# Attention's value product: key tile 0 in two blocks of 256 queries, a wait for masks at each block, query projection one unit sooner

## The reference, cut to what matters

```python
q = (x @ Wq + bq).reshape(Bb, Ss, H, HD)
k = (x @ Wk + bk).reshape(Bb, Ss, H, HD)
v = (x @ Wv + bv).reshape(Bb, Ss, H, HD)
scores = jnp.einsum('bthd,bshd->bhts', q, k) / jnp.sqrt(jnp.asarray(HD, x.dtype))
scores = scores + alibi[None]
scores = jnp.where(causal[None, None], -jnp.inf, scores)
attn = jax.nn.softmax(scores, axis=-1)
out = jnp.einsum('bhts,bshd->bthd', attn, v).reshape(Bb, Ss, Dd)
return out @ Wo + bo
```

## Time and profile before

| what | value |
|---|---|
| median of 3 runs | 937.36 us (935.0, 937.36, 949.56) |
| the profiled execution's own time | 934.77 us |
| its span, first to last instruction | 933.1 us |
| PE busy | 828.5 us (89%), 6498 matmuls |
| DVE busy | 752.8 us (81%) |
| ACT busy | 640.4 us (69%) |
| POOL busy | 537.4 us (58%) |
| mean granted TensorE clock | 0.951 |

### The profile page before, as it was taken

The page is one execution under the profiler, slowest core; times in us unless marked ns, Lnnn a source line. Parts: engine busy times, 40 slices in busy tenths (PEclk is TensorE's granted clock), DMA queues, the critical chain, the costliest instruction groups (busy, mean ns, idle before and its releaser), DMA issues. The chain is left out here.

```text
span 933.1 us, 23978 instructions
## 1 busy us (share of the span) xinstructions
PE 828.5 (89%) x6498; PEld 383.2 (41%) x6498; DVE 752.8 (81%) x2534; ACT 640.4 (69%) x1538; POOL 537.4 (58%) x838
## 2 busy tenths in 40 slices
PE   4999999359899999999999999999999977999997
PEld 3444444124334444444434444444444334444443
DVE  3899988348788888988988988888899416999996
ACT  3776666211687778778778778777877844766775
POOL 3677777431654654655565565475453323778787
PEclk9999999655899999999999999999999997999999
DMA  6500000042221322232232232132221001000101
GB/s 165 106 0 0 0 0 0 34 153 87 99 94 65 124 104 69 104 108 80 85 122 82 70 134 91 62 121 103 73 101 36 2 3 22 28 30 26 30 26 43
DMA packets 57044, 62.50 MB, mean 67 GB/s; under 512 B 6752, under 2 KB 50656, under 8 KB 56864
## 3 DMA queue, kind: packets, MB, share of 16 engines
q1 hardware_dynamic: 56992, 61.86, 20.5%
HBM read 32.23 MB, written 29.36 MB: 66 GB/s over the span
## 5 line engine op out<-in xcount | busy, mean ns | idle before, releaser
L1094 DVE TENSOR_REDUCE att_neg_max<-att_max 128x1 bf16<-128x512 f32 (+3 forms) x704 | 414.5, 638 | 61.8 <-PE att_max L888 59.5
L987 ACT ACTIVATE att_probs<-att_exp 128x512 f32<-128x512 f32 x640 | 357.6, 596 | 102.4 <-PE att_exp L907 98.5
L1059 POOL TENSOR_SCALAR_AFFINE_SELECT att_probs<-att_probs 128x512 f32<-128x512 f32 x256 | 159.0, 634 | 240.9 <-ACT att_probs L987 240.8
L907 PE MATMUL att_exp<-att_q_st,att_k_st 53*128 53x512 bf16 (+3 forms) x1024 | 223.0, 302 | 0.6 <-ACT att_probs L987 0.6
L885 PE MATMUL att_max<-att_k_st,att_q_st 51*128 51x384 bf16 (+2 forms) x768 | 191.2, 285 | 19.4 <-DVE att_neg_max L1094 11.4
L923 PE MATMUL att_pv<-att_probs,att_v 128*32 128x512 f32 (+3 forms) x2048 | 191.8, 448 | 2.7 <-POOL att_probs L1059 2.4
L360 ACT ACTIVATE moe_scaled<-moe_hi,moe_gates 128x128 f32<-128x128 f32 x512 | 145.7, 371 | 61.4 <-PE moe_hi L306 61.0
L520 DVE SCALAR_TENSOR_TENSOR x<-moe_lo,moe_gates,x 128x128 f32 (+1 forms) x512 | 160.7, 339 | 20.3 <-PE moe_lo L300 19.2
L888 PE MATMUL att_max<-att_k_st,att_q_st 64*128 64x128 bf16 x1024 | 176.0, 224 | 0.0
L885 PEld LDWEIGHTS att_max<-att_k_st,att_q_st 51*128 51x128 bf16 x768 | 71.1, 95 | 216.4 <-DVE att_neg_max L1094 159.1
L300 PE MATMUL moe_lo<-moe_we,moe_hT 128*128 128x512 f32 x256 | 136.0, 613 | 0.0
(11 more groups left out here) (81 smaller groups left out, 872.1 us busy)
## 6 DMA issues: line engine op xcount, KB each, us to landing
qk_parts<-att_parts SPq DMA_DIRECT2D x32, 384.0 KB, 2.7
att_q_st<-qk_parts SPq DMA_DIRECT2D x64, 192.0 KB
att_k_st<-qk_parts SPq DMA_DIRECT2D x64, 192.0 KB
qk_parts<-att_parts SPq DMA_DIRECT2D x32, 256.0 KB, 2.1
x<-in_L_attn_x SPq DMA_DIRECT2D x16, 256.0 KB, 2.9
qk_parts<-att_parts SPq DMA_DIRECT2D x32, 128.0 KB, 1.7
out<-x SPq DMA_DIRECT2D x16, 256.0 KB, 2.3
moe_we<-in_L_ffn_We SPq DMA_DIRECT2D x2, 512.0 KB, 4.9
```

What stands on the lines that cost most here:

```text
L907: mm = nc.tensor.matmul(exp_ps[m % RING][:, c:c + S - j * P], k_st[par][low:low + FINE_ROW, r, j * P:(j + 1) * P], q_st[par][low:low + FIN ...
L987: nc.scalar.activation(probs[g % 2][:, n, :], exp_ps[m % RING][:], ACT.Exp).then_inc(exp_done, 1)
L1059: nc.gpsimd.affine_select(out=view, in_=view, compare_op=ALU.is_ge, fill=0.0, base=0, pattern=[[0, 4], [1, P]], channel_multiplier=-1).the ...
L1094: nc.vector.tensor_reduce(neg_max[par][:, g // 2, 1 - g % 2, heads[0]:heads[0] + len(heads), i], max_ps[m % RING][:, 0:len(heads) * width] ...
```

## The change

The block of key tile 0 (512 queries) becomes two blocks of 256: queries 0 to 255 behind unit 2 and 256 to 511 behind unit 3. The first block of each key tile waits for `masked` up to the number in `MASKED_FOR`: 1 for key tile 0, 3 for tile 1, 4 for tile 2, 3 for tile 3; the second block of key tile 0 has no wait. Only the very first matmuls (key tile 0, queries from 0, first head of a pair) have the start flag. `project_q` goes from unit 2 to unit 1 of group 0. Nothing else changes.

```diff
 SIDE_WORK = [
-    {2: "project_q", 4: "shift_hi", 8: "project_k"},
+    {1: "project_q", 4: "shift_hi", 8: "project_k"},
...
-PV_AFTER = {3: 0, 5: 1, 7: 2, 9: 3}
+
+PV_AFTER = {2: (0, 0, 2), 3: (0, 2, 4), 5: (1, 1, 4), 7: (2, 2, 4), 9: (3, 3, 4)}
+MASKED_FOR = [1, 3, 4, 3]
...
-                            on_pv(b, par, g - 1, PV_AFTER[n])
+                            on_pv(b, par, g - 1, *PV_AFTER[n])
                         if g == 0 and there(b - 1):
-                            on_pv(b - 1, 1 - par, GROUPS - 1, PV_AFTER[n])
+                            on_pv(b - 1, 1 - par, GROUPS - 1, *PV_AFTER[n])
...
-            def weigh_values(b, par, g, j):
+            def weigh_values(b, par, g, j, q0, q1):
 
                 half_at, ab = divmod(g, 2)
-                if j == 0:
-                    pe.wait_ge(masked, b * NK + (g + 1) * MASK_UNITS)
+                if q0 == j:
+                    pe.wait_ge(masked, b * NK + g * MASK_UNITS + MASKED_FOR[j])
+                if j == 0 and q0 == 0:
                     if ab == 0 and (g > 0 or after(b, 0)):
                         pe.wait_ge(pv_read, b * HALVES + half_at)
                     if g == 0:
                         pe.wait_ge(side_read, use(b - 1, "project_v"))
                 for hh in range(4):
                     n, c = next((n, c) for n in range(EXP_UNITS) for h, jj, c in exp_unit(n) if (h, jj) == (hh, j))
-                    mm = nc.tensor.matmul(pv_ps[VW * hh:VW * (hh + 1), j * P:S], v[par][:, j, 4 * half_at + hh, ab, :],
-                                          probs[g % 2][:, n, c:c + S - j * P], start=(ab == 0 and j == 0),
-                                          stop=(ab == 1 and j == T - 1))
+                    mm = nc.tensor.matmul(pv_ps[VW * hh:VW * (hh + 1), q0 * P:q1 * P], v[par][:, j, 4 * half_at + hh, ab, :],
+                                          probs[g % 2][:, n, c + (q0 - j) * P:c + (q1 - j) * P],
+                                          start=(ab == 0 and j == 0 and q0 == 0), stop=(ab == 1 and j == T - 1))
                 if j == T - 1:
                     mm.then_inc(pv_out, 1)
...
-            def copy_values(b, par, g, j):
+            def copy_values(b, par, g, j, q0, q1):
```

## The result

The changed kernel takes 950.0 us (median of 4 runs, 948.87 to 950.83), the kernel before on the same chip 936.18 (4 runs). The ratio is 1.0179, 95% interval 1.0151 to 1.0207: slower by about 16.7 us, where I had forecast 8.7. The ratio leaves out one execution of the kernel before (949.56) that ran in the chip's slower state; the median of all four has it in. The profiled execution took 950.72 us with a span of 949.0, against 934.77 and 933.1.

A forecast was written before the change was run, and what follows sets the result against it. The prediction took PE to set the pace in groups 0, 1 and 3 and DVE in group 2. Its terms, 9.9 - 0.9 + 0.7 - 1.0 = +8.7 us on 934.8, gave 943.5 us, range 932 to 951.

The forecast's parts named there:

- split, walks 0 to 14: Key tile 0's two half blocks on PE: 0.66 us a walk in groups 0, 1 and 3, 9.9 us over 15 walks.
- masks in group 1: Unit 3 to its block in group 1: 0.09 us of mask waiting goes in about 10 walks, -0.9 us.
- more waits: Own waits for key tiles 1, 2 and 3 on PE's queue: taken as 0, with 0.09 kept for the range.
- `project_q`: Query projection behind unit 1 instead of 2 in group 0: same matmul between the same neighbours, cost 0.
- last walk and end: Last walk pays +0.66 us in three groups; at the end key tile 0 moves into the mask wait, -1.0 us.
- +0.22 us a group on PE: Units 2 and 3 with key tile 0's block go from 1.54 to 1.76 us; group 2's stall absorbs it.
- The waits show (slower): Three more waits a group on PE's queue cost 0.09 us each, 17.3 us over 192, giving 964; chance 0.07.
- no stall worth a row: Groups 1 and 3: PE's blocks follow each other without notable stall, so PE sets the pace from unit 2 on.
- Rows 1: The page's strip over attention, slices 10 to 32: read as PE at 9 in every slice, clock granted in full.
- Every group pays: Group 2 pays too, so all 64 groups cost 0.22 us: +12.2, 947 us; chance 0.12.
- nearly free: The half blocks' fixed part overlaps its neighbours, so only the gains stay: 933 us; chance 0.09.
- evening out: Parting projection and long block in group 0 ends DVE's 0.95 us of waits a walk: 929 us; chance 0.12.

The follow-up runs named there:

- slots 0 and 40: Changed kernel with PE's loop loaded so its first instruction is number 0 or 40 of a block of 256 instructions: 932.18 us and 931.98 us.
- `project_q` alone: Kernel before with only the query projection moved from behind unit 2 to behind unit 1: 933.78 us, ratio 0.9999.
- slot 236: Kernel before, only PE's loop loaded to start at instruction 236 of a block of 256: 943.13 us, ratio 1.0132.
- finer waits alone: Kernel before with each key tile waiting for its own masks; key tile 0 one block behind unit 3, query projection at unit 2: 927.05 us, ratio 0.9915.
- the kernel before with its loop written out: Kernel before with PE's loop over walks written out, so no jump back, and nothing else: 929.65 us, ratio 0.9964.
- slot 64: Changed kernel, only PE's loop loaded to start at instruction 64 of a block of 256: 939.68 us, ratio 1.0086.
- the split with one wait: Changed kernel without separate mask waits: key tile 0's first block waits behind unit 2 for all four masks: 964.43 us, ratio 1.0334.
- the run with the loop written out: Changed kernel with PE's loop over walks written out, other engines still in loops: 931.69 us, ratio 0.9979.

## Why the prediction was wrong

The time of 950.0 lies within the range, near its end, but for another reason than any case in it, so that it lies there is luck. The forecast and what the traces show, in us (walks are counted by the sequence whose values they weigh; all terms but the code's compare the kernel before with the change at slots 0 and 40):

| term | forecast | measured |
|---|---|---|
| split, walks 0 to 14 (measured: 1 to 14) | +9.9 | +4.7 |
| masks in group 1 | -0.9 | 0 |
| masks at the start (walk 0) | none | -3.7 |
| more waits | 0 | 0 |
| `project_q` (the walk ahead of walk 0 alone) | 0 | +0.2 |
| last walk and end | -0.3 | -0.9 |
| **code fetched at the jump back** | **none** | **+18.2** |
| sum in attention | +8.7 | +18.5 |

From the first max unit to the last value product attention takes 582.3 us instead of 563.8. Between the two profiled executions it also began 2.4 us sooner (195.6 instead of 198.0); the run of the change at slot 0 begins at 198.1 and that of `project_q` alone at 195.8, so that is no part of the change. 18.5 - 2.4 gives the 16 us between them.

**The step that failed** is the price of the split, "+0.22 us a group on PE", and with it the whole sum, which has no term for added instructions but the time that they run. "More waits ... only its handling on PE's queue counts" has the same gap, though its 16 instructions alone did no harm (927.05 us). 128 of the 144 added to the loop's body are the split's. What the runs showed in its place is 18.2 us at four jumps back, which go away (932.18) when the same body is loaded at another place. The order that I had read showed the growth (the query projection stood at 879 and now at 893, although it comes a unit sooner; the last products at 1755 and now at 1806). No rival held it. The rival "The waits show (slower)" had the right direction and the wrong mechanism: the leads before key tiles 1 to 3 did not grow (mostly 0.40, 0.32 to 0.37 and 0.21 us, before and after). The Trainium skill ("Runtime: NRT & Kernel Launch", section "Instruction fetch mechanics") says that PE's instruction memory holds 2048 instructions in blocks of 256, fetched ahead in sequence, and that a taken branch out of the current window of two pages costs a fetch. I had not weighed it. The runs agree with the eight blocks and with the block's size (258 instructions a packet). They speak against the two pages: seven blocks stayed through every jump at slots 0 and 40.

**The split** cost half of the forecast. Its parts are as predicted; here PE in group 2 and group 3 of an undisturbed walk with the change (slot 0):

```profile
452.10 0.33 PE L888 MATMUL att_max<-att_k_st,att_q_st 51*128 51x384 bf16 x1
...
452.42 0.64 PE L927 MATMUL att_pv<-att_probs,att_v 128*32 128x256 f32 x8
452.99 0.33 PE L888 MATMUL att_max<-att_k_st,att_q_st 51*128 51x384 bf16 x1
...
453.88 0.28 PE L888 MATMUL att_max<-att_k_st,att_q_st 51*128 51x256 bf16 x1
...
454.53 0.28 PE L888 MATMUL att_max<-att_k_st,att_q_st 51*128 51x256 bf16 x1 [0.25 <-DVE att_neg_max L1098]
...
462.86 0.28 PE L888 MATMUL att_max<-att_k_st,att_q_st 51*128 51x256 bf16 x1
...
463.04 0.27 PE L888 MATMUL att_max<-att_k_st,att_q_st 51*128 51x256 bf16 x1
```

A block of 256 columns takes 452.99 - 452.42 = 0.57, with a lead of 0.32. In group 2 the stall before unit 5 went from 0.39 to 0.25, and the group's time stayed 8.94, as predicted. In group 3 unit 4 to unit 5 takes 463.04 - 462.86 = 0.18. The kernel before has there

```profile
462.74 0.28 PE L885 MATMUL att_max<-att_k_st,att_q_st 51*128 51x256 bf16 x1
...
463.06 0.28 PE L885 MATMUL att_max<-att_k_st,att_q_st 51*128 51x256 bf16 x1
```

0.32: a stall of 0.14 in front of DVE, which I passed over as "no stall worth a row". The rows of the matmuls don't name it, but the weight load ahead of the second one does:

```profile
463.06 0.09 PEld L885 LDWEIGHTS att_max<-att_k_st,att_q_st 51*128 51x128 bf16 x1 [0.20 <-DVE att_neg_max L1094]
```

It absorbs most of 0.22. In group 1 the same step goes from 0.35 to 0.19. Measured by group in the steady walks: +0.24, 0, 0 and +0.07, together 0.31, where I had +0.22, +0.13, 0 and +0.22. DVE paces all groups but 0 more nearly than I took it to.

**The masks.** The 0.09 in group 1 brought nothing: with finer waits alone the walk is 33.71 as before. There unit 3 to unit 4 of group 1 falls from 1.40 to 1.31, and unit 4 to unit 5 grows from 0.35 to 0.44: the stall in front of DVE took it up. But of the two waits for masks in rows 3 I used the one of 1.47 and never looked for the other. It stands before the first value product of all, in the kernel before:

```profile
240.87 1.93 PE L923 MATMUL att_pv<-att_probs,att_v 128*32 128x512 f32 x8 [0.98 <-POOL att_probs L1059]
```

and around it before, then after (windows from 240 and from 236 us):

```profile
240.00:248.00 8.00, 7.13 (x46) 2.93 (x48) 3.29 (x7) 2.38 (x5) 4.92 (x7) 0.57 0.41 145
```

```profile
236.00:244.00 8.00, 7.64 (x94) 3.59 (x95) 7.11 (x14) 5.78 (x12) 7.55 (x11) 1.00 0.43 151
```

A wait of 0.98 us was followed by a clock of 0.57 in these 8 us, in which PE did half as many matmuls. Rows 1 had a sign of it that I misread: slice 11, 233 to 257 us, has an 8 for PE and an 8 for the clock, where I wrote 9 in every slice and the clock granted in full. With the change PE doesn't stand still there, the clock stays at its upper level, and walk 0 takes 32.2 us instead of 35.9. With the finer waits alone it takes 32.0, and the same product starts without a wait and is done in 1.07 instead of 1.93:

```profile
238.26 1.07 PE L926 MATMUL att_pv<-att_probs,att_v 128*32 128x512 f32 x8
```

The size isn't the same in every execution. In the trace of slot 0 the clock rises only at 239.9 us, instead of at 230 to 234 as in the others, and walk 0 takes 33.6; in that of the kernel before with its loop written out the dip behind the wait lasts 3.4 us instead of 6.8, and it takes 34.6.

**The end** gave 0.9 net, where the forecast had 0.3: three groups of the last walk pay 0.24 each, as forecast, its group 0 becomes 0.19 shorter, and the tail behind POOL's last mask 1.44 shorter instead of 1.0. After (PE, then POOL):

```profile
775.18 2.81 PE L926 MATMUL att_pv<-att_probs,att_v 128*32 128x128 f32 x48
```

```profile
775.21 1.81 POOL L1062 TENSOR_SCALAR_AFFINE_SELECT att_probs<-att_probs 128x512 f32<-128x512 f32 x3 [2.07 <-ACT att_probs L990]
```

POOL's last mask ends at 777.02, PE's products at 777.99: 0.97 behind it. Before it was 761.84 - 759.43 = 2.41. Not only key tile 0 but also key tile 1 (0.78) no longer waits for the last mask, which is key tile 2's. `MASKED_FOR` says 3 of the 4 for key tile 1, and I had used it for tile 0 alone.

**The rivals.** "Every group pays" and "the waits show" are refuted by the groups' times, "nearly free" was half right about the split, and "evening out" did not happen (group 0 pays the full 0.24, and `project_q` alone brings nothing). With the loop at slot 0 or 40 the whole change comes to 0 within 0.25%: what the split costs, the finer waits give back.

## What to carry to other kernels

Before adding instructions inside a loop on one engine, count its body in code blocks of 256 and note where it begins: a loop that grew from seven code blocks to eight lost 18 us. Its place alone can do it too, as the kernel before at slot 236 shows, so code added ahead of the loop would be enough. The signs are the queue for instructions on the page and a few long waits for "issue" one loop pass apart; placing the loop's head, a hint for the jump, or writing the loop out takes them away. And follow every row of a wait to its place, above all a short one before which PE's clock is full and behind which it isn't.

## What the runs showed of the hardware

- A jump back on PE costs next to nothing to a body in 7 code blocks (0.5 us from matmul to matmul, no packet of code after the first pass), and 3.0 to 4.0 us from matmul to matmul when a ninth has been fetched before it. A second wait can follow, 2.22 us in the run of before at slot 236.
- In the changed kernel every stall was followed by 3.4 to 6.8 us at the lower clock level, in the kernel before at slot 236 by 10.2 us. A single stall with all that follows cost 4.7 us with the head at slot 64 (two walks of 37.54 and 35.23 against 34.02 each) and 7.9 us in the kernel before at slot 236 (36.81 and 38.50 against 33.71).
- With few instructions in the eighth code block (3 or 31) one jump in four stalled in the profiled executions, with 139 all four. The change at its natural place and the split with one wait also stalled at all four; how far their bodies reach into the eighth isn't on record. Why the fetch of the ninth comes earlier or later is open.
- Code that runs straight on is fetched with no stall (23 packets in 270 us), beside data transfers that keep the DMA engines 27% busy (the run with the loop written out).
